# Four postnorm layers on one core: state inputs and outputs merged over both channel halves, spread rows in two pairs of PSUM banks, and a new order of the calls

## What is computed

```
xz = x @ in_proj.T;  x_in, z = halves(xz)
x_conv = silu(causal depthwise conv(x_in))
B, C, s = x_conv @ x_proj.T              # 16, 16 and 1 rows per token
dt  = softplus(s * dt_w + dt_b)
dA  = exp(dt * A[n]);  dBx = dt * B[n] * x_conv
h[n] = dA * h[n] + dBx                   # over time, 16 states n
y   = sum over n of h[n] * C[n]
out = (y * silu(z)) @ out_proj.T
```

## Time and profile before

| | |
|---|---|
| median of 3 runs | 1095.97 us (1095.84 to 1096.62) |
| profiled execution, its own time | 1098.24 us |
| its span, first to last instruction | 1096.0 us |
| instructions | 8799 |
| mean granted TensorE clock | 0.871 of full |

### The profile page before, as it was taken

One profiled execution on the slowest core, in us unless ns is written; L12 is line 12 of the kernel. 1 busy time (PEld: TensorE's weight loads), 2 busy tenths in 40 slices (PEclk: granted clock), 3 DMA queues, 4 the chain that ended last, 5 costly groups with the idle time before them and its releaser, 6 DMA issues. The chain is left out here.

```text
span 1096.0 us, 8799 instructions
## 1 busy us (share of the span) xinstructions
PE 819.7 (75%) x2536; PEld 500.2 (46%) x2536; DVE 857.7 (78%) x1226; ACT 607.3 (55%) x983; POOL 581.6 (53%) x419
## 2 busy tenths in 40 slices
PE   1358559736976997799869988899779889269376
PEld 0226226323643654465526563557346646145244
DVE  0302314999799999999999999998999899999811
ACT  3533545754666676667575767565853574534221
POOL 2041251567556864778285838683656474654410
PEclk9769769866988999899898998899889989569678
DMA  8000000000000010001000010001000000000000
GB/s 306 0 19 20 0 20 19 1 0 19 1 0 1 1 58 1 0 1 59 0 1 0 1 58 0 1 1 39 1 0 1 20 1 1 19 0 1 19 0 20
DMA packets 9215, 19.43 MB, mean 18 GB/s; under 512 B 1360, under 2 KB 3920, under 8 KB 9168
## 3 DMA queue, kind: packets, MB, share of 16 engines
q1 hardware_dynamic: 9168, 18.88, 5.0%
HBM read 14.68 MB, written 4.19 MB: 17 GB/s over the span
## 5 line engine op out<-in xcount | busy, mean ns | idle before, releaser
L334 POOL TENSOR_TENSOR y<-y,hC 128x1024 f32<-128x1024 f32 x112 | 285.7, 2551 | 57.4 <-DVE hC L902 54.1
L1075 PE MATMUL pC<-w,hT 128*128 128x256 f32 x1024 | 234.7, 384 | 16.1 <-ACT hT L532 16.0
L594 ACT ACTIVATE dA<-dt,A_neg 128x512 f32<-128x512 f32 x256 | 174.7, 719 | 122.4 <-DVE hs L889 122.2
L1188 PE MATMUL pBC<-stack,sel 97*128 97x512 f32 x256 | 158.1, 636 | 95.5 <-DVE hs L889 94.9
L1075 PEld LDWEIGHTS pC<-w,hT 128*128 128x128 f32 x1024 | 195.9, 192 | 52.9 <-issue 18.6
L876 DVE TENSOR_TENSOR pBC<-u,pBC 128x512 f32<-128x512 f32 x256 | 164.6, 687 | 43.6 <-PE pBC L1188 42.4
L902 DVE TENSOR_TENSOR hC<-hs,pBC 128x512 f32<-128x512 f32 x256 | 160.9, 669 | 1.5 <-PE pBC L1188 1.5
L889 DVE TENSOR_TENSOR_SCAN hs<-dA,carry,pBC 128x512 f32<-128x512 f32 x128 | 156.2, 1261 | 0.0
L889 DVE TENSOR_TENSOR_SCAN hs<-dA,pBC 128x512 f32<-128x512 f32 x128 | 148.5, 1200 | 0.0
L532 ACT ACTIVATE hT<-pA,ffb_sb 128x512 f32<-128x512 f32 x128 | 86.4, 687 | 101.6 <-PE pA L1068 101.4
L1188 PEld LDWEIGHTS pBC<-stack,sel 97*128 97x128 f32 x256 | 52.8, 206 | 163.4 <-DVE hs L889 138.9
(11 more groups left out here) (106 smaller groups left out, 1084.1 us busy)
## 6 DMA issues: line engine op xcount, KB each, us to landing
xt<-xT SPq DMA_DIRECT2D x8, 515.0 KB, 4.9
xtok<-x SPq DMA_DIRECT2D x8, 512.0 KB, 4.7
out<-x3b SPq DMA_DIRECT2D x8, 512.0 KB, 2.8
w<-w1a SPq DMA_DIRECT2D x1, 1024.0 KB, 9.5
w<-w2a SPq DMA_DIRECT2D x1, 1024.0 KB, 11.3
w<-w1b SPq DMA_DIRECT2D x1, 1024.0 KB, 8.2
w<-w2b SPq DMA_DIRECT2D x1, 1024.0 KB, 9.9
gate_w<-gateT SPq DMA_DIRECT2D x1, 512.0 KB, 7.5
```

What stands on the lines that cost most here:

```text
L334: nc.gpsimd.tensor_tensor(y[:], so_far, hC[:, n % CRING, :, :], ALU.add).then_inc(S["y_sum"], 1)
L594: nc.scalar.activation(dA[:, k % ARING, :], dt[:, h, :], ACT.Exp, scale=A_neg[:, h, n:n + 1]).then_inc(S["dA_ready"], 1)
L1075: mm = nc.tensor.matmul(dst[:, b * D:b * D + D], src(k, t0), w[:, k, :], start=k == 0, stop=k == nk - 1)
L1188: return nc.tensor.matmul(dst[:], sel[0:NXK, row:row + 1].to_broadcast([NXK, P]), stack[ch[1]][0:NXK, :], start=True, stop=True)
```

## The change

- The eight banks are divided anew. pM is gone. Rows and inputs have two pairs of banks, taken in turn by states: in a pair the first bank takes the input of the first half and later row C, the second bank row B and then the input of the second half.
- `state_input` is one instruction of 128x1024 for both halves, with row B repeated; `state_output` likewise with row C. The scans stay apart, and become two calls.
- The order puts the output of a state behind the first scan of the next; output 15 is done in the following step, and with it the sum on GpSimd. Input 0 is done at the end of the step before.
- What used pM now uses pA0 and pA1, and so has to wait for the gate and up matmuls' readers there.
- The calls of all four engines are in a new order. Chunks are described by a small class (`ch.i`, `ch.T`, `ch.nb`), all still of 512, so that shapes stay as they were but for the merged ones. An increment of a semaphore *passed*, which stood before some instructions, is gone. The DMAs' sizes and waits are the same.

```diff
-        pM = bank("pM")
-        pBC = [bank(f"pBC{n}") for n in range(BRING)]
+        pS = ctx.enter_context(nc.psum_tensor("pS", [P, 2, H, T], F32))
+        def inputs(n):
+            return pS[:, n % 2, :, :]
+        def C_bank(n):
+            return pS[:, n % 2, 0, :]
+        def B_bank(n):
+            return pS[:, n % 2, 1, :]
...
             def state_input(ch, n):
-                else:
-                    dve.wait_ge(S["hC_ready"], UNITS * c + H * n)
+                if NS * c + n >= 2:
+                    dve.wait_ge(S["hC_ready"], NS * c + n - 1)
                 dve.wait_ge(S["B_mm"], NS * c + n + 1)
-                for h in range(H):
-                    V.tensor_tensor(input_banks(n)[h][:], u[ch[1]][:, h, :], B_bank(n)[:], ALU.mult).then_inc(S["dBx_ready"], 1)
+                V.tensor_tensor(inputs(n)[:, :, 0:ch.T], u[ch.side][:, :, 0:ch.T],
+                                B_bank(n)[:, 0:ch.T].unsqueeze(1).to_broadcast([P, H, ch.T]), ALU.mult).then_inc(S["dBx_ready"], 1)
...
             def state_output(ch, n):
-                for h in range(H):
-                    dve.wait_ge(S["h_ready"], UNITS * c + H * n + h + 1)
-                    V.tensor_tensor(hC[:, n % CRING, h, :], hs[:, n % HRING, h, :], C_bank(n)[:], ALU.mult).then_inc(S["hC_ready"], 1)
+                dve.wait_ge(S["h_ready"], UNITS * c + H * n + H)
+                V.tensor_tensor(hC[:, n % CRING, :, 0:ch.T], hs[:, n % HRING, :, 0:ch.T],
+                                C_bank(n)[:, 0:ch.T].unsqueeze(1).to_broadcast([P, H, ch.T]), ALU.mult).then_inc(S["hC_ready"], 1)
...
             def spread_B(ch, n):
-                if not (first(ch) and n == 0):
-                    pe.wait_ge(S["h_ready"], UNITS * c + H * (n - 1) + (1 if n else H))
+                if NS * c + n >= 2:
+                    pe.wait_ge(S["h_ready"], UNITS * c + H * (n - 1))
             def spread_C(ch, n):
-                if n > 0:
-                    pe.wait_ge(S["h_ready"], UNITS * c + H * n)
-                elif not first(ch):
-                    pe.wait_ge(S["hC_ready"], UNITS * c)
+                pe.wait_ge(S["h_ready"], UNITS * ch.i + H * n + 1)
...
-            def dt_row(ch):
-                pe.wait_ge(S["stack_ready"], num(ch) + 1)
-                spread(pM, ch, 2 * NS).then_inc(S["s_mm"], 1)
+            def dt_row(ch, gate):
+                if gate is not None:
+                    pe.wait_ge(S["relu0"], FB * gate.i + FB - 1)
+                pe.wait_ge(S["stack_ready"], ch.i + 1)
+                spread(pA[0], ch, 2 * NS).then_inc(S["s_mm"], 1)
...
-            def x1_transpose(ch, h, tail):
+            def x1_transpose(ch, h, prep, tail):
+                if h == 0 and prep is not None:
+                    pe.wait_ge(S["stack_ready"], prep.i + 1)
```

More of the change, by code:

```diff
@@ L49 @@
 ARING = 4
-BRING = 3
 ADDS = NS - 1
@@ L184, in chunk @@
             def chunk(i):
-                return (i // PER_SEQ, i % PER_SEQ) if 0 <= i < NCHUNK else None
+                return CHUNKS[i] if 0 <= i < NCHUNK else None
             for i in range(LAG_AHEAD, NCHUNK + LAG_TAIL):
                 step(*(chunk(i - lag) for lag in LAGS))
[L190 to L200, removed]
         @block.sync
@@ L241, in step @@
                     load(ahead)
-                    if first(ahead):
+                    if ahead.i == 0:
                         load_weights()
@@ L701, in step @@
                 if gate is not None:
-                    relu(0, gate, 0, tail)
                     relu(0, gate, 1)
                     relu(0, gate, 2)
-                if gate is not None:
                     relu(0, gate, 3)
+                if ahead is not None:
+                    conv_tap(ahead, 2, prep)
                 if scan is not None:
@@ L1133, in up, with down @@
                 if f >= 2:
                     pe.wait_ge(relu, FB * c + f - 1)
-                channel_major(pA[f % 2][:], w1[layer], f * P, lambda k: xT_[:, k, :], done)
-            def down(layer, ch, j, b):
+                channel_major(ch, pA[f % 2][:], w1[layer], f * P, lambda k: xT_[:, k, :], done)
+            def down(layer, ch, j, b, gate=None, prep=None, tail=None):
                 relu, done = ((S["relu0"], S["down0_mm"]), (S["relu1"], S["down1_mm"]))[layer]
+                if 2 * j + b >= ch.nb:
+                    return
@@ L1139, in down @@
                 weight(ch, f"w2_{layer}")
-                pe.wait_ge(relu, FB * num(ch) + FB)
+                if layer == 0 and tail is not None:
+                    pe.wait_ge(sum_ready[LN_OUT], PAIRS[tail.i + 1])
+                if layer == 1 and gate is not None:
+                    pe.wait_ge(S["o_scaled"], BLOCKS[gate.i + 1])
+                elif layer == 1 and prep is not None:
+                    pe.wait_ge(S["zz_ready"], H * (prep.i + 1))
+                pe.wait_ge(relu, FB * ch.i + FB)
@@ L1348, in step @@
                     up(0, gate, 7)
+                if prep is not None:
+                    dt_row(prep, gate)
+                if scan is not None:
+                    spread_C(scan, 14)
+                if prep is not None:
+                    spread_B(prep, 0)
+                if gate is not None:
+                    down(0, gate, 0, 0, tail=tail)
                 if scan is not None:
```

868 lines of the change are left out of this document (449 added, 419 removed).

## The result

The changed kernel takes **1020.87 us** (median of 4 runs, 1019.5 to 1021.63) against 1096.15 for the kernel before beside it: ratio 0.9312, 95% interval 0.9295 to 0.9328. The profiled execution has its own time of 1020.38 us and a span of 1018.6.

What follows compares the result with a forecast made beforehand. VectorE was taken to set the pace, TensorE close behind. From 1098.24 us: merging -15, spread-row waits -42, contention -10, new waits +36, fill +2, less 2.27 for the median, gave 1067 us; range 1036 to 1091.

Steps and rivals of the forecast that it cites:

- the waits for spread rows: VectorE waiting for rows B and C in 24 places; two bank pairs and later outputs would save 42 us.
- Contention: VectorE scans slowed beside GpSimd: log A's part saved, -10 us, ends -20 and 0; the recurrence would stay slow.
- What is late next: New waits at dt row and u, v, down-projection and out-projection, carries and y ring: +36 us, between 10 and 50.
- It fits with nothing to spare: Chain before u of relu, table load and softplus: 3.4 us against 3.3 before; charged 2.5 us a step, 15 in all.
- the out-projection: TensorE's group of 16 matmuls, 6.42 us after 5.94 idle: idle mostly gone and the group near 3.6 us.
- Merging, -15 us: State inputs and outputs merged from two halves: 0.12 us saved in each of 128 states, -15 us.
- the bare state: A state with nothing of another stage in it on VectorE: 4.74 us expected, 4.86 before.
- each merge saves a whole overhead: Rival for merged inputs and outputs: 41 us saved in all, 26 more than the forecast, time 1041 us; chance 0.03.
- Fill and drain: First u some 3.5 us later, less about 2 for an earlier root; drain keeps its chain: +2 us.
- few new waits: Rival: the new order has spare time, new waits +10 instead of +36 us, time 1041 us; chance 0.14.
- TensorE as the new bound: Rival: TensorE's 97 us a step stretch, new waits reach 50 us, contention stays, time 1091 us; chance 0.14.
- the dt chain: Last up matmul, dt row and softplus before u; rival that it runs slower, 1108 us at 8 a step; chance 0.08.

Runs made afterwards that it cites:

- The three runs above: Changed kernel with row B released behind the previous state's last scan, 1253.73 us; outputs behind their own scans, 1163.55; state 0's row B behind first down-projection blocks, 1047.75.
- The runs with narrow sums: GpSimd's y sums for states 2 to 15 cut to 16 columns: kernel before 1072.58 us, changed kernel 1014.66; kernel before with conv sums cut too, 1059.37.
- the moved recurrence: Changed kernel with recurrence behind output 6, 1041.36 us; kernel before with output 6 moved behind the recurrence, 1087.64 us.
- the first run: Changed kernel with each state's merged input and merged output both cut in two again, new order kept: 1015.99 us.
- the second: Changed kernel with the inputs alone cut in two, outputs left merged: 1012.65 us.
- run 40: Not a run's number: 40 is a time in us, said of the first run, the changed kernel with inputs and outputs cut in two, 1015.99 us.
- one call moved: Changed kernel with ScalarE's step sizes (softplus of the next chunk) put behind the last conv tap: 1047.74 us.
- the runs whose waits came back: Changed kernel with outputs directly behind their own scans, 1163.55 us, and with row B held for the previous state's last scan, 1253.73 us.

## Why the prediction was wrong

**The bound and the waits for spread rows** were right. VectorE set the pace and still does; -42 forecast, -41 seen (43.9 us for rows B and C before, 3.1 after, counting the 1.5 for outputs). The three runs above show that this term hangs on both parts of the edit and on the seam.

**Contention** was the first step that failed, at the sentence "The recurrence stays beside GpSimd's work": -10 us forecast, at most -20, where the eight forms lost 44. I had reasoned that GpSimd idles until output 3 in the block of log A, which held (1263 ns), but did not carry the same rule to output 6, which the change puts behind the recurrence, although I named that very wait of GpSimd's under the new waits for v. Moving that one call back costs 20 us. Nor did I count u, v, tg and 1 - a squared, whose means in the old trace were well above their time alone too. The runs with narrow sums and the moved recurrence show GpSimd's work as the cause for the recurrence, log A, tg, u, the clip and xi; for v and 1 - a squared it is read from what overlaps them in the timelines.

**"What is late next", +36 us,** was the second. Of its four points: u waits nothing after the fill (15 charged), v 0.8 (9), the down-projections 1.9 (8), carries 2.3 (4): 5 in all, plus 6.0 for x3b that no point named. "It fits with nothing to spare" was nearly so, 1.0 us; the failed step is the charge of 2.5 us a step for it, a wait put where there was only a lack of room. The same with TensorE: at the higher clock it had 9 us of each step free, and the out-projection took 3.69 us after 0.84 idle, as the prediction said it might:

```profile
533.16 3.69 PE L1102 MATMUL pC<-out_w,st 128*128 128x256 f32 x16 [0.84 <-DVE st L845]
```

What the higher clock was worth by itself no run isolates.

**Merging, -15 us,** was mis-sized and mis-named. I had taken the hand-over costs (0.03 and -0.08) from pairs of halves and the pair of scans, and the bare state came out at 4.80 instead of 4.74. The larger error is the factor of 128: a bare state is not the typical one. What the new order saves, the hand-over from output to input, 0.12 us with its overlap, was there in only 37 states, some -4 us; the run with everything cut in two has this order and no merges, and its bare state of 4.74 would have made -15. By VectorE's time in and between its state instructions, waits for others left out, the states as a whole went from 605 to 602 us: -3. The merges alone cost 5 us by the first run, and the merged input alone 8 by the second.

The Trainium skill says ("VectorE: DVE Perf Modes", The DRAIN you can't avoid) that the next instruction does not start until the pipe is empty. Read as in the prediction, so that each merge saves a whole overhead, it would make the first run 40 us slower, and that was 5 faster. The same paragraph adds what the prediction left out, that an instruction that is not held starts earlier, and the trace agrees: 0.07 to 0.10 us before the one ahead ends.

**Fill and drain** (+2) moved by about 1 us each: the first u starts at 174.39 instead of 173.65, and the drain is 1.0 shorter. With the terms as measured, 1098.2 - 3 - 41 - 44 + 11 makes 1021; the profiled execution took 1020.4.

Of the rivals, *few new waits* was the case, with contention beyond its bounds on top. TensorE as the new bound (0.14) was the opposite of what happened: with its stalls gone it was busy for 788.0 us instead of 819.7.

## What to carry to other kernels

When an order of calls is changed, look for each call that another engine waits for, and note what now runs before it: that engine's idle gap was worth as much here as the waits that went (44 and 41 us), because what runs in the gap runs alone. Merge two instructions only where neither neighbour then depends on the whole, and count how often that pair really stands together before multiplying a bare state's gain. And a chain that just fits, as the dt chain did with 1.0 us to spare, costs nothing; past that point it is dear (27 us for one call moved), for a late call also lands beside other work.

## What the runs showed of the hardware

- VectorE's instructions with two inputs in SBUF take up to about two and a half times their time beside GpSimd's 128x1024 additions and products (u 1.22 to 3.12 us, a scan 1.26 to 3.30), and GpSimd's take 3.25 for 2.37. Some with one input in SBUF do so too: 1 - a squared (mean 671 to 1410 ns), the clip of the decays and the copies of xi. State scans, inputs and outputs, with one operand in PSUM, read nearly the same in every run (1261 to 1275 ns for the 128x512 scans with a carry). The Trainium skill ("SBUF — State Buffer", Who interferes with whom) says that a VectorE instruction with two SBUF inputs contends with a GpSimd instruction that reads SBUF, one with at most one such input only in its two-port modes. By that the trace agrees for the first kind; whether the forms with one input ran in such a mode no view names. The rule was at hand; what I failed to do was to apply it to each call's new place.
- An independent VectorE instruction starts 0.07 to 0.10 us before the one ahead ends; one that needs it starts 0.03 after a multiplication (output to input, before), 0.09 (merged input to scan) or 0.14 (scan to merged output).
- TensorE's granted clock over the whole kernel is lower where it stalls more: 0.897 in the change, 0.854 and 0.831 in the runs whose waits came back, and the same 2536 matmuls took 788, 846 and 857 us. So a wait for TensorE that is removed may give more than itself; by how much no run isolates.
